# A fused cross-attention and mixture-of-experts kernel: the order of the work behind the last token tile, the engine that makes five tiles' gates, and the place of one mask bias

## The reference

```python
x = x + tanh(g_xattn) * xattn(layernorm(x), ctx)     # 16 heads of 16, causal and padding mask
x = x + tanh(g_ffn)  * ffn(layernorm(x))
# ffn: a router picks one of 8 experts for each token
router_probs = softmax(xt @ Wr + br)
gates = max(router_probs);  idx = argmax(router_probs)
xn = layernorm(xt) * ln_g + ln_b
h = relu(xn @ W1[idx] + b1[idx])                     # 256 -> 1024
y = (h @ W2[idx] + b2[idx]) * gates                  # 1024 -> 256
```

## Time and profile before

| | us |
|---|---|
| median of 3 runs | 305.45 |
| lowest and highest run | 304.74 and 310.8 |
| the profiled execution, its own time | 305.7 |
| its span, from the first to the last instruction | 303.9 |
| busy PE, DVE, ACT, POOL in the span | 278.6, 196.3, 165.9, 155.2 |

### The profile page before, as it was taken

One profiled execution on the slowest core, in us unless ns is written; L12 is line 12 of the kernel. 1 busy time (PEld: TensorE's weight loads), 2 busy tenths in 40 slices (PEclk: granted clock), 3 DMA queues, 4 the chain that ended last, 5 costly groups with the idle time before them and its releaser, 6 DMA issues.

```text
span 303.9 us, 7807 instructions
## 1 busy us (share of the span) xinstructions
PE 278.6 (92%) x2512; PEld 248.7 (82%) x2512; DVE 196.3 (65%) x638; ACT 165.9 (55%) x444; POOL 155.2 (51%) x298
## 2 busy tenths in 40 slices
PE   7899999999999999999887899999999999999960
PEld 3668898988888789987576898999888899989960
DVE  4478589998988899888729945664355433344530
ACT  3243466776666667676544644876428344544440
POOL 2426246888888888644776152485312442314240
PEclk9999999999999999999669999999999999999995
DMA  6999993010104454643231031311111111110310
GB/s 154 289 310 371 376 379 130 35 38 35 37 36 150 159 159 156 225 150 122 72 116 62 2 107 54 106 61 54 54 40 54 50 57 57 54 53 23 91 61 14
DMA packets 19855, 34.63 MB, mean 114 GB/s; under 512 B 2518, under 2 KB 14612, under 8 KB 19801
## 3 DMA queue, kind: packets, MB, share of 16 engines
q1 hardware_dynamic: 15513, 21.28, 21.7%
q0 software_dynamic: 4144, 12.62, 13.2%
q10 hardware_dynamic: 144, 0.07, 0.1%
HBM read 27.60 MB, written 6.75 MB: 113 GB/s over the span
## 4 chain that ended last, share of the span: by engine, by line
PE 57%; POOL 17%; DVE 12%; issue 6%; DMA 2%; ACT 1%; SPq 1%; POOLq 1%; DVEq 1%; ACTq 0%
PE pS L1811 20%; PE pB L1885 14%; PE pB L1587 4%; PE pB L1607 3%; PE pA L1497 3%; PE pT L1497 3%; DVE mx L919 2%; DMA cst<-in_consts_dram 2%; POOL W2s L423 2%; POOL b L425 2%; POOL mv L375 2%; POOL mv L390 2%; POOL xs L381 2%; POOL rows_dram L412 2%; DVE Pb L927 1%
## 5 line engine op out<-in xcount | busy, mean ns | idle before, releaser
L1811 PE MATMUL pS<-znf,W1c 128*128 128x128 f32 x576 | 72.9, 281 | 3.3 <-ACT znf L740 1.7
L1811 PEld LDWEIGHTS pS<-znf,W1c 128*128 128x128 f32 x576 | 68.7, 195 | 6.8 <-issue 4.5
L1885 PE MATMUL pB<-W2p,hT 128*128 128x256 f32 x408 | 53.6, 285 | 1.6 <-DVE hT L1286 1.3
L448 POOL DMA_INDIRECT out_dram<-yo,idxs x17 | 17.9, 1053 | 67.8 <-DVE yo L1307 57.7
L1885 PEld LDWEIGHTS pB<-W2p,hT 128*128 128x128 f32 x408 | 49.5, 189 | 3.5 <-DVE hT L1286 1.5
L1279 DVE TENSOR_SCALAR hA<-pS,b1s 128x128 f32<-128x128 f32 x72 | 20.3, 344 | 45.8 <-PE pS L1811 39.4
L762 ACT ACTIVATE hA<-pS,b1s 128x128 f32<-128x128 f32 x72 | 20.5, 367 | 44.1 <-PE pS L1811 33.0
L1587 PE MATMUL pB<-VB,PT 128*128 128x51 f32 (+1 forms) x320 | 39.4, 271 | 1.7 <-DVE xs L949 1.7
L1587 PEld LDWEIGHTS pB<-VB,PT 128*128 128x128 f32 (+1 forms) x320 | 38.1, 192 | 3.3 <-issue 3.0
L624 ACT ACTIVATE Pb<-Pb 128x616 f32<-128x616 f32 x32 | 23.0, 717 | 19.2 <-DVE Pb L927 19.0
L431 POOL DMA_INDIRECT zin<-rows_dram,idxg x21 | 21.7, 1032 | 15.7 <-issue 12.4
(11 more groups left out here) (271 smaller groups left out, 505.2 us busy)
## 6 DMA issues: line engine op xcount, KB each, us to landing
W1s<-in_L_ffn_W_dram SPq DMA_DIRECT2D x8, 1024.0 KB, 9.7
W2s<-in_L_ffn_W_dram SPq DMA_DIRECT2D x8, 1024.0 KB, 11.3
rows_dram<-pay POOLq DMA_DIRECT2D x16, 260.0 KB, 2.4
xs<-in_x_dram SPq DMA_DIRECT2D x3, 512.0 KB, 7.5
W2s<-in_sel_dram SPq DMA_DIRECT2D x1, 385.0 KB
zin<-rows_dram,idxg POOLq DMA_INDIRECT x21, 3.4
out_dram<-yo,idxs POOLq DMA_INDIRECT x17
W1s<-in_L_xattn_wk_dram SPq DMA_DIRECT2D x1, 256.0 KB, 3.1
```

The lines of the kernel that those rows point to most:

```text
L1811: t = e.matmul(pS[:, 2 * (s % 2) + n, 128 * c:128 * c + 128], W1c[k][n][:, 128 * c:128 * c + 128], znf[s % 2][:, 128 * k:128 * k + 128], s ...
L1885: t = e.matmul(o, hT[s % 2][a][:, 128 * c:128 * c + 128], W2p[b_][c // 2][:, D * (c % 2):D * (c % 2) + D], start=False, stop=(c == 7 and a ...
```

## The change

Four things are different.

1. Gates of tiles 4 to 8 are made by DVE (a reciprocal and a product, at the end of iterations 7 to 11), no longer by POOL. `Lg` has three buffers in place of two, and the logits of tile i wait for the gate of tile i-3.
2. POOL stores the rows of tiles 9 to 12 one iteration later than before; the last of them behind the loop, ahead of the first gather.
3. `mask_bias(1)` stands in iteration 1 of DVE's loop.
4. Behind the last tile the order is another on PE, ACT, DVE and POOL, the five `warm` matmuls ahead of `transpose_z(0)` are gone, and the low parts of chunks 2 and 3 of slot 0's W2 are made by DVE.

```diff
-WARM = (6, 3, 4, 5)
+WARM = (6, 3, 4)
+GATES_DVE = range(4, 9)
-        Lg = sbt("Lg", [128, 2, 4, E])
+        Lg = sbt("Lg", [128, 3, 3, E])
...
 POOL
             def store_row(i):
-                gate(i)
-                e.wait_ge(g["pool_gate"], i + 1)
+                if i not in GATES_DVE:
+                    gate(i)
+                e.wait_ge(*gated(i))
...
-                if n >= 3:
+                if 3 <= n < 12:
                     store_row(n - 3)
+                elif n > 12:
+                    store_row(n - 4)
...
             y, z = NT - 2, NT - 1
+            store_row(y - 2)
             e.wait_ge(g["dve_idxg"], 1)
...
             gather(1)
+            rstd2(z)
             gather(2)
-            rstd2(z)
             store_row(y - 1)
...
-            W2_low(0, 2, r_new[0][0])
-            W2_low(0, 3, r_new[0][0])
...
 ACT
             x2_row(y)
+            copy_OT(z)
             e.wait_ge(g["dve_slot"], 1)
             regs(0)
...
             W1_copy(0, 0, 0)
-            copy_OT(z)
             W1_copy(0, 1, 0)
-            W1_copy(0, 0, 1)
-            W1_copy(0, 1, 1)
             gate_exp(y - 1)
             z_row(y)
             gate_exp(y)
-            W2_high(0, 0)
             e.wait_ge(g["dve_lnb"], 1)
             layer_in(0)
+            W1_copy(0, 0, 1)
+            W1_copy(0, 1, 1)
+            for c in range(4):
+                W2_high(0, c)
             x2_row(z)
-            W2_high(0, 1)
-            layer_in(1)
             z_row(z)
             gate_exp(z)
-            W2_high(0, 2)
-            W2_high(0, 3)
+            layer_in(1)
+            regs(1)
             e.wait_ge(g["dve_b1"], 1)
             relu(0)
             high(0, 0)
-            regs(1)
...
 DVE
             def logits(i):
                 e.wait_ge(g["pool_r"], i + 1)
-                if i >= 2:
-                    e.wait_ge(g["pool_gate"], i - 1)
+                if i >= 3:
+                    e.wait_ge(*gated(i - 3))
...
+            def gate(i):
+                L3 = Lg[:, i % 3, 2, :]
+                e.wait_ge(g["act_ge"], i + 1)
+                e.reciprocal(L3[:, 4:5], L3[:, 1:2]).then_inc(g["dve_own"], 1)
+                if i >= 3:
+                    e.wait_ge(rsem[i % 3], 16 * (i // 3))
+                e.wait_ge(g["dve_own"], own.up())
+                e.tensor_scalar(pay[:, i % 3, 512:513], L3[:, 4:5], tg[:, 1:2], None, ALU.mult).then_inc(
+                    g["dve_gate"], 1)
...
                 if n == 1:
                     poison()
-                if n == 3:
                     e.wait_ge(g["dve_pois"], 1)
                     mask_bias(1)
...
+                if n - 3 in GATES_DVE:
+                    gate(n - 3)
...
+            norm(z)
             t_taken = first_slots()
-            norm(z)
...
+            together(rank(1))
             e.wait_ge(g["dve_slot"], 1)
             regs(0)
...
             logits(z)
-            together(router(z), rank(1))
-            W2_low(0, 0)
-            W2_low(0, 1)
+            together(router(z))
+            for c in range(4):
+                W2_low(0, c)
             regs(1)
             W1_copies(1)
-            e.wait_ge(g["dve_b1"], 1)
-            relu(0)
             more = rank(2)
...
 PE
             project(z)
+            ranks(1)
+            counts(1)
             first_bias()
-            warm(WARM[3], pS[:, 3, :])
             transpose_z(0)
             hidden(0, 0)
             transpose_z(1)
-            ranks(1)
-            counts(1)
-            hidden(0, 1)
             counts(2)
             ranks(2)
+            hidden(0, 1)
             slot(0)
```

27 lines of the change are left out of this document (18 added, 9 removed).

## The result

The changed kernel took 302.31 us (median of 4 runs, 301.09 to 303.88) against 306.53 us for the kernel before in the same set. The ratio is 0.9887, with a 95% interval of 0.9841 to 0.9932. The same kernel was timed twice more among the experiments: 0.9828 [0.9786, 0.987] and 0.9880 [0.984, 0.992]. The mean of the three is 0.9865, some 4.1 us. The forecast was 6.7 us: its sign is right and its size is more than half as large again as what was measured. All three medians (302.31, 301.13, 301.57) lie inside the range of the prediction, and outside the 298.2 to 300.0 of its likeliest case. The executions of one kernel come in a faster and a slower state, and a ratio compares the faster ones alone, so it is not quite the quotient of two medians.

A forecast was written before the change was run, and what follows sets the result against it. POOL was taken to set the loop's pace, DVE next, and PE's waits and fillers the passage behind it. 1.35 + 2.6 + 1.2 + 0.95 + 0.6 = 6.7 us off 305.7 gave 299.0 us, range 296.7 to 303.2.

The forecast's parts named there:

- likeliest case: The whole kernel at 298.2 to 300.0 us, around the forecast of 299.0; chance 0.45.
- The gates: Tile loop, iterations 7 to 11: gates moved to DVE free POOL and DVE sets the pace; gain 1.35 us.
- rival 1: Tile loop: POOL operations hold DVE's in four iterations, so the loop gives -0.6 us; 301.0 us, chance 0.14.
- The mask and the first gather: Mask bias moved to iteration 1, and later stores ahead of the first gather: both covered by waits, 0 us each.
- The fillers: Passage behind the last tile: five filler matmuls go and two short PE waits shrink; gain 2.6 us together.
- rival 2: Passage: PE's clock comes back one half later, losing time on hidden(0, 1); 301.0 us, chance 0.14.
- The tick: Passage: two DVE waits go, its tick comes 3.9 us earlier; PE gains 1.2 of its 1.45 us wait.
- The low part: Passage: without POOL's low parts of W2, DVE makes h's low part sooner; gain 0.95 of PE's 1.26 us wait.
- The collecting matmuls: Passage: PE's wait ahead of the matmuls collecting the later slots' rows shrinks; gain 0.6 of 0.75 us.
- Rival 4: Passage: ACT's queue ends each step in DVE's place, leaving only lower bounds; 302.4 us, chance 0.16.
- Rivals 3 and 5: 3: clock stays down through slot 0, 306.5 us, chance 0.04; 5: clock never falls, 297.9 us, chance 0.07.

The follow-up runs named there:

- e12: The changed kernel with VectorE's gate split, the reciprocal ahead of the router's x part and the product behind it; ratio 0.9835 to the kernel before.
- e8: The kernel before, repeated with no edit for a second profile; 303.11 us in one run.
- e15: The kernel before, repeated with no edit for a third profile; 305.39 us in one run.
- e9: The changed kernel, timed a third time with no edit; 301.57 us, ratio 0.9880 to the kernel before.
- e11: The changed kernel with slot 3's gather behind the stores and four filler matmuls where PE waits ahead of z's transposes and projection; 299.31 us, ratio 0.9825.
- e1: The changed kernel, timed a second time with no edit; 301.13 us, ratio 0.9828 to the kernel before.
- e16: The changed kernel with 16 empty instructions in VectorE's queue ahead of z's residual; 301.19 us in one run.
- e7: The changed kernel with the last two low parts of slot 0's W2 back on POOL, behind its stores; ratio 0.9970 to the kernel before.
- e5: The changed kernel with POOL's gather for slot 3 behind the stores of rows 14 and 15; ratio 0.9829 to the kernel before.

## Why the prediction came out as it did

**The gates: right, 0.25 us too much.** 1.11 us against 1.35. POOL's time dropped out and VectorE's counts, as said, and rival 1 did not come: the five reciprocals take 0.15 us each and the five products 0.21. The term was mis-sized by the price of a gate: 0.29 us was read from a pair on four columns; here a gate takes 0.39 us of VectorE's queue and makes an iteration 0.34 us longer (7.42 for 7.08). Five times 0.05 is the 0.25. With the product moved away from the reciprocal (e12) the iteration is 0.14 us shorter.

**The mask and the first gather: right,** 0.07 us and nothing visible.

**The fillers: this is the step that failed.** The text says "in this execution the fillers did not bring the clock back, and I take it that it comes back by the end of hidden(0, 0) as before". Both are right for that execution. The error was to price the passage by it alone: the fillers as 2.29 us of loss and nothing else, and with them VectorE's 2.79 us of waiting for the ranks behind the slow half as time to be won. In four of five executions with the old order on PE the half ran at full clock behind the fillers; in e8 and e15 the tick came 26.86 us behind the scores of tile 15 (28.60 in the first profile) and output(0) 31.00 (32.70). The typical kernel before is 1.7 us better there than the execution that was read. Without fillers the half started 2.2 to 2.4 us earlier (2.6 forecast for them and the short waits) and ran at the lower clock every time, so 1.55 to 1.74 us went back into it. Against the executions e8 and e15 the passage gains 2.26 us (1.10 in e9) up to output(0), against 3.8 forecast. Against the first profile it gains 3.96: that the forecast of these two terms fits the first pair of profiles is the luck of the draw. In its effect this is rival 2 (one half at the lower clock that would not be), with its place one half earlier. But the changed kernel's slow half is not what holds its output(0): in e11 the half took 2.05 us and output(0) stood at the same place, since VectorE's tick did. Only where the lower clock outlasts the half does it show: in e9 the next 32 matmuls took 4.76 us for 4.08, and output(0) came at 29.90.

**The tick: right in its two reasons, and its size was that of one execution.** Both of VectorE's waits fell away, and PE's wait of 1.28 to 1.45 us with them, but for 0.18 us in e1 and 0.20 in e16. The tick came 3.98 us earlier than in the first profile (24.62 for 28.60, with 3.9 forecast), and 2.24 us earlier than in e8 and e15.

**The low part: right in its size.** The 1.26 us within output(0) are gone, in the first profile as in e8. The stretched products of VectorE are gone with them. That POOL's low parts of W2 stretched them fits the rows of both profiles, 1.21 and 1.25 us in one and 1.43 and 1.24 in the other, but no run separates it; e7 shows another cost of those parts, PE's wait for POOL's own product.

**The collecting matmuls: wrong.** 0.6 us were to be won, and in the first profile 0.9 were lost (1.67 for 0.75); from output(0) to output(1) the gain is 0.6 to 0.7 us where the low part and this term together had 1.55 (1.87 in e9, whose output(0) was late itself). The text held that "only a landing over 0.5 us late would be seen", and did not work out how late it would be. POOL came to its third gather 1.64 us later than before (24.84 us behind the scores of tile 15 for 23.20); 0.75 of that is its product for row 13, 1.06 us for 0.31 beside VectorE's low parts of W2. Row 15's own product was stretched too. The store went out at 29.96 us (28.92 in the first profile, 28.12 in e8), and ACT came to it at 30.92, where in e8 it was not there before 35.19. So ACT waited 1.46 us. e5 puts the store ahead of the gather, and the wait falls to 0.24. The prediction's last paragraph had named such a wait among the signs of being wrong.

**The sum.** Forecast 6.7; a loop of 1.18 and a passage of 2.9 give 4.1, which is what the three sets of runs have in the mean. What is missing is 0.25 in the gates, some 1.6 us by which the typical kernel before is better than the one that was read, and 0.6 to 0.8 at the store, 2.5 to 2.65 us together for the 2.6. Rival 4 was near in its number (302.4) and wrong in its mechanism: it was one wait of ACT, not its whole queue. Rivals 3 and 5 did not occur; rival 3's argument that PE would have "no pause over 0.5 us" was wrong all the same, for the 0.96 us ahead of the half stayed.

## What to carry to other kernels

A profile is one execution: where a term rests on a stretch at the lower clock, look at a second profile first, because work that looks useless in one (fillers whose successor is slow anyway) may pay in most, and another engine's wait behind that stretch is of the same draw. When an engine's queue gets later, work out the landing of the last transfer in it, and put stores that someone waits for ahead of gathers that nobody needs yet. Fillers cost nothing where the engine waits anyway: four of them there left the start of the half where it was (18.83 us for 18.93), five in the path put it 1.3 us later (20.25). Whether they gain anything there is not shown.
